# Loads and products ahead of the first P tile in another order, and three quantiser groups moved behind it

## The chip, the cores and the metric

One core of one Trainium2 chip runs the whole program. The metric is the device time of one execution in microseconds (us).

## What is computed

For 8 sequences of 256 tokens with 1024 features (float32), the reference adds two layers to `x`, one after the other:

```python
# layer 0: quantised input, then a routed low-rank layer (4 experts, rank 16)
xq = dequantised x        # 8 thresholds; each has its own delta and zero point
logits = xq @ router_w.T                                  # 4 experts, top 2, softmax over the two
mid = einsum('tf,erf->ter', xq, A)
x = x + einsum('te,teo->to', gates, einsum('ter,eor->teo', mid, B) * 4)
# layer 1: x @ W.T plus a rank-32 part picked by a label, then K, a bias and two low-rank parts
h = einsum('bsi,oi->bso', x, W) + einsum('bsr,or->bso', einsum('bsi,bir->bsr', x, lora_A[label]), B_w) * 0.5
A_eff, B_eff = einsum('bn,nri->bri', gate, LA), einsum('bn,nor->bor', gate, LB)   # 16 LoRAs mixed per sequence
x = x + h @ K + bias + B_eff (A_eff h) + B_shared (A_shared h)
```

## The kernel before

The products that don't depend on `x` are folded first. K' is K plus the shared low-rank update (A_shared by B_shared, rank 32). P is the identity plus W.T times K', 1024 by 1024, kept in SBUF as a high and a low float32r part, so that each product is three passes (high by high, low by high, high by low). With P at hand, each tile of `x` needs one large product and a few thin ones.

**Stages.** (1) The head: small products that mix the LoRA factors. `la` (LoRA A, 4 parts `g`) times the gate matrix gives `aefft` (L814, copied out at L502); `bw` times `aefft` is the bw product, in `cbank` (L824), from which VectorE makes `cbd` (L731); `ab` holds the shared factors, split into a high part by ScalarE (L492) and low parts by VectorE (L712, L713); `k_update` (L796) multiplies them into a ring of three banks and `k_add` (L647) adds each to the loaded K in `kst`; `kp_split` (L431) and `kp_lo_part` (L652) split K'; `v_product` (L806) is `bw` times K'; `lb` (LoRA B, 4 parts, two halves each) times the gate matrix gives 8 table products (L839), which `rows_out` (L488) copies to `tst` and SP stores to `t_dram`. (2) The P loop, `STEPS` = 16 tiles in two halves of 8. In the first half each tile is preceded by a u product (L896, L898), copied out as `ust` (L537). Each tile needs `w_hi` (ScalarE, L424) and `w_lo` (VectorE, L639) of its W tile and ends in `p_hi` (L525) and `p_lo` (L745). K' of the second half is made beside the first half, and split at tile 8. (3) The x loop, 64 slots, two for each tile of 128 tokens by 512 columns.

**The quantiser** runs beside (1) to (3): 8 chunks (sequences) `c` of 8 groups `g`. For each group ScalarE makes the levels (L395) of the *next* group and raises its own (L406); VectorE clips (`value`, L598), makes a mask (L608) and merges (L615); the first group of a chunk has no merge, the last no mask but a `finish` (L620). ScalarE takes |x| once for each chunk (`magnitude`, L387), behind group 1. A raise from group 3 on waits for the merge two groups back, and that of group 1 of a later chunk for all merges of the chunk before. After a chunk, TensorE runs `mid(c)` (L848) in `midbank`, VectorE ranks the experts (`order`, L679 ff.) and makes the gates (`gate`, L695 ff.), TensorE turns them (`gated_turn`, L858) and ScalarE copies the result (`gated_out`, L446).

**What sets the order.** Each engine runs its own instructions in the order written; semaphores join them. All groups stand in a list `ORDER`; the first `AHEAD` are written out by hand in the head and the others are laid into slots (16 of the P loop, 64 of the x loop) by the table `TAKEN`. `DONE[c]` is the slot of a chunk's last group, and `mid`, `order`, `gate` and the turn stand a fixed number of slots behind it (`LAGS`). On ScalarE the groups of slot n+1 come behind `ust(n)` and `p_out(n-1)` of slot n, and ahead of the `w_hi` of slot n+1. On VectorE slot n holds `k_add`, `w_lo`, `p_lo`, the groups of slot n, then ranks and gates. Loads come from SP's queue in the order written, `x` for the quantiser from POOL's (L284).

Of the kernel before, what the change touches and what calls it, by code (L numbers as in the profile page):

```python
# [36 lines left out]
BATCH = 8  # L37
# [3 lines left out]
KT = D // P  # L41
# [17 lines left out]
WARM, WARMUPS = 256, 9  # L59
# [4 lines left out]
def build(nc, a, out_t, itok):  # L64
    arena = [(nc.sbuf_base + 31) // 32 * 32]

    def place(name, shape, dt, at=None, after=0):
# [93 lines left out]
    consts_in, lb_in, ab_in, bw_in, itok_in, alt_in, ra_in = (  # L161
        sem(n) for n in ("consts_in", "lb_in", "ab_in", "bw_in", "itok_in", "alt_in", "ra_in"))
# [12 lines left out]
    t_stored, v_moved = [sem("t_stored0"), sem("t_stored1")], sem("v_moved")  # L175
# [26 lines left out]
    N_CONST = 3  # L202
# [5 lines left out]
    AHEAD = 5  # L208
# [64 lines left out]
    with nc.allow_non_contiguous_dma(reason="rows of 1 KB and small constants"), nc.Block() as block:  # L273

        @block.gpsimd
        def _(pool):

            def quant_input(c):
                if c == 1:
                    pool.wait_ge(lb_in, 16)  # L280
                if c >= 2:
                    pool.wait_ge(levels_made, (c - 1) * G)
                    pool.wait_ge(abs_made, c - 1)
                pool.dma_start(xq[:, c % 2], x_v[c]).then_inc(xq_in[c % 2], 16)  # L284

            for c in range(BATCH):
# [3 lines left out]
        def _(sp):  # L290
            sp.dma_start(small, a["small"]).then_inc(small_in, 16)
            sp.dma_start(ab_raw, a["ab"]).then_inc(ab_in, 16)
            for g in range(NG):
                sp.dma_start(la[:, g], a["la"][:, g]).then_inc(lora_in[g], 16)
            sp.dma_start(bw, a["bw"]).then_inc(bw_in, 16)
            for i in range(KPARTS):
                sp.dma_start(kst[:, i * KO:(i + 1) * KO], k_v[0, :, i * KO:(i + 1) * KO]).then_inc(k_part_in[i], 16)
            for n in range(2):
                sp.dma_start(wst[n], w_v[n]).then_inc(w_in[n], 16)
            sp.dma_start(lb, a["lb"]).then_inc(lb_in, 16)  # L300
            for dst, name in ((bdmask, "bdmask"), (ident_raw, "ident"), (before, "before")):
                sp.dma_start(dst, a[name]).then_inc(consts_in, 16)
            sp.dma_start(itok_sb, itok).then_inc(itok_in, 16)
            sp.dma_start(ra, a["ra"]).then_inc(ra_in, 16)
            sp.wait_ge(itok_in, 16)
            label = [sp.value_load(itok_sb[0:1, b:b + 1], min_val=0, max_val=LAB - 1) for b in range(BATCH)]
            for b in range(BATCH):

                sp.dma_start(alt[b % BG * R:(b % BG + 1) * R, b // BG],
                             a["alt"][bass.ds(label[b], 1)].rearrange("o r i -> (o r) i")).then_inc(alt_in, 16)  # L310
            sp.wait_ge(kp_hi_made, KT)
# [3 lines left out]

            for g in range(NG):
                sp.wait_ge(t_made, 2 * (g + 1))
                sp.dma_start(t_dram[g * RG:(g + 1) * RG].rearrange("r b d -> (r b) d"), tst[0:2 * R, g % 2]).then_inc(t_stored[g % 2], 16)
# [13 lines left out]
            for m in range(2, LOADS):  # L332
# [7 lines left out]
                if m == KT + 2:  # L340

                    for s in range(2):
                        sp.wait_ge(t_stored[s], 16 * NG // 2)
                    sp.wait_ge(kfull, HALVES * KT)
                    sp.wait_ge(v_made, HALVES)
                    for s in range(2):
                        sp.dma_start(tb[R:2 * R, s], tst[3 * R:4 * R, 0]).then_inc(v_moved, 16)
# [35 lines left out]
        def _(act):  # L383
# [5 lines left out]
            def levels(c, g):  # L389

                if g == 0:
                    act.wait_ge(xq_in[c % 2], 16 * (c // 2 + 1))
# [33 lines left out]
            def kp_split(h):  # L426
                for o in range(KT):
                    act.wait_ge(k_sum, h * KT + o + 1)
# [4 lines left out]
            def v_rows(h):  # L433
                act.wait_ge(vfull, h + 1)
                nc.scalar.activation(tst[3 * R:4 * R, 0, h * HALF:(h + 1) * HALF], misc[3 * R:4 * R], ACT.Copy,
                                     scale=LORA1).then_inc(v_made, 1)
# [27 lines left out]
            def bp_out(s):  # L464

                for h in range(HALVES):
                    act.wait_ge(bpfull, h + 1)
                    act.wait_ge(v_moved, 32)
# [13 lines left out]
            def rows_out(n):  # L482
# [3 lines left out]
                if g >= 2 and h == 0:  # L486
                    act.wait_ge(t_stored[g % 2], 16 * (g // 2))
                nc.scalar.activation(tst[0:2 * R, g % 2, h * HALF:(h + 1) * HALF], obank[n % RING][0:2 * R],  # L488
                                     ACT.Copy).then_inc(t_made, 1)

            act.wait_ge(ab_in, 16)
            nc.scalar.activation(ab, ab_raw, ACT.Copy).then_inc(ab_hi_made, 1)  # L492
            act.wait_ge(tables, 1)
            levels(0, 0)
# [531 lines left out]
```

## Time and profile before

| what | us |
|---|---|
| median of 3 runs | 488.16 |
| lowest and highest | 486.01, 490.64 |
| the profiled execution | 489.24 |
| its span in the trace | 487.5 |
| TensorE busy | 471.8 |
| VectorE busy | 391.4 |
| ScalarE busy | 356.6 |

The profile shows one execution. Its engines are PE (TensorE matmuls), PEld (their weight loads), DVE (VectorE), ACT (ScalarE), POOL and SP, which only issues transfers. A float32 matmul shows as two instructions, a float32r one as one. The granted clock (PEclk) is the share of full speed that TensorE's clock was allowed. The time of an execution is some 2 us longer than the span of its trace.

### The profile page before, as it was taken

Reading aid. Unit: us, or ns where it says so; the run is one execution under the profiler, and the core shown is the slowest. Engines: PE = TensorE matmul, PEld = TensorE weight load, DVE = VectorE, ACT = ScalarE, POOL = GpSimd, SP = SyncE. Lnnn points to the kernel's source line nnn. Section 1 sums busy time; section 2 is a strip of 40 time slices with the busy share of each in tenths; the row PEclk is TensorE's granted clock in tenths of the full one; section 3 lists DMA queues with packets and bytes.
Section 4 is the critical chain, followed back from the end, with each engine's and each line's share of the span. In section 5 each row is a group of like instructions: output and inputs, shape, how many; then the busy total and the mean of one; then the engine's idle time right before and its main releaser. Section 6 shows DMA issues by size and latency. Waiting matters only on the chain.

```text
span 487.5 us, 5645 instructions
## 1 busy us (share of the span) xinstructions
PE 471.8 (97%) x2200; PEld 365.7 (75%) x2200; DVE 391.4 (80%) x381; ACT 356.6 (73%) x297; POOL 6.8 (1%) x12
## 2 busy tenths in 40 slices
PE   6989999999889999999999999999999999999896
PEld 5963788887648888787777777787787768767774
DVE  3289978789979989939879989798799994999400
ACT  3779987864978398676699599776899697776001
POOL 0000000001000001000000000000000000000000
PEclk9599999999999999999999999999999999999799
DMA  8975542313301527030441316014214013102002
GB/s 281 422 267 178 171 142 73 90 43 98 107 0 37 181 86 204 13 108 1 151 141 44 108 54 200 38 55 130 108 54 152 0 55 129 56 0 86 1 0 87
DMA packets 35500, 50.61 MB, mean 104 GB/s; under 512 B 26610, under 2 KB 26866, under 8 KB 33074
## 3 DMA queue, kind: packets, MB, share of 16 engines
q1 hardware_dynamic: 34322, 41.87, 26.7%
q0 software_dynamic: 1152, 8.39, 4.8%
q8 instruction: 17, 0.28, 0.2%
q14 instruction: 9, 0.07, 0.1%
HBM read 39.51 MB, written 10.49 MB: 103 GB/s over the span
## 4 chain that ended last, share of the span: by engine, by line
PE 76%; DVE 16%; issue 4%; DMA 2%; ACT 1%; SPq 0%; DVEq 0%; ACTq 0%
PE bank L965 10%; PE bank L966 10%; PE bank L967 10%; DVE val L615 7%; PE bank L848 6%; PE bank L942 5%; PE bank L874 5%; PE bank L917 5%; PE bank L913 5%; PE bank L914 4%; PE bank L896 3%; DVE inside L608 3%; PE bank L814 3%; DVE val L598 2%; DMA la<-la_in 2%
## 5 line engine op out<-in xcount | busy, mean ns | idle before, releaser
L406 ACT ACTIVATE val<-level,shift,small 128x2048 f32<-128x2048 int16 x64 | 133.8, 2091 | 16.3 <-DVE val L615 16.2
L615 DVE COPY_PREDICATED val<-inside,val 128x2048 f32<-128x2048 uint8 x56 | 141.3, 2523 | 0.3
L395 ACT ACTIVATE level<-xq,inv 128x2048 int16<-128x2048 f32 x64 | 127.9, 1998 | 2.0 <-DMA xq<-xt_in 1.4
L598 DVE TENSOR_SCALAR val<-val,width,unshift 128x2048 f32<-128x2048 f32 x64 | 86.0, 1347 | 22.7 <-ACT val L406 22.4
L965 PE MATMUL bank<-p_hi,x_hi 128*128 128x512 f32 x256 | 102.5, 401 | 0.0
L966 PE MATMUL bank<-p_lo,x_hi 128*128 128x512 f32 x256 | 100.4, 392 | 0.0
L967 PE MATMUL bank<-p_hi,x_lo 128*128 128x512 f32 x256 | 100.4, 392 | 0.0
L608 DVE TENSOR_SCALAR inside<-absx,thr 128x2048 uint8<-128x2048 f32 x56 | 71.4, 1285 | 7.1 <-ACT absx L387 7.1
L965 PEld LDWEIGHTS bank<-p_hi,x_hi 128*128 128x128 f32 x256 | 48.5, 189 | 17.6 <-issue 8.8
L966 PEld LDWEIGHTS bank<-p_lo,x_hi 128*128 128x128 f32 x256 | 48.4, 189 | 10.5 <-issue 0.5
L967 PEld LDWEIGHTS bank<-p_hi,x_lo 128*128 128x128 f32 x256 | 48.3, 189 | 10.5
L913 PE MATMUL bank<-kp_hi,w_hi 128*128 128x512 f32 x128 | 50.8, 397 | 1.8 <-DVE kp_lo L652 1.8
L917 PE MATMUL bank<-kp_hi,w_lo 128*128 128x512 f32 x128 | 50.4, 393 | 0.0
L914 PE MATMUL bank<-kp_lo,w_hi 128*128 128x512 f32 x128 | 49.9, 390 | 0.0
L848 PEld LDWEIGHTS bank<-ra,val 128*128 128x128 f32 x256 | 31.5, 202 | 3.0 <-DVE val L620 1.7
L848 PE MATMUL bank<-ra,val 128*128 128x68 f32 x256 | 31.5, 284 | 1.3 <-DVE val L620 1.3
L942 PE MATMUL bank<-tb,zt 128*128 128x512 f32 x64 | 32.7, 599 | 0.0
L896 PE MATMUL bank<-aefft,wst 128*128 128x256 f32 x128 | 29.1, 380 | 2.2 <-ACT ust L537 2.2
L874 PE MATMUL bank<-xs,ub 128*64 128x256 f32 x128 | 29.3, 382 | 0.0
L896 PEld LDWEIGHTS bank<-aefft,wst 128*128 128x128 f32 x128 | 24.1, 190 | 6.9 <-issue 3.4
L913 PEld LDWEIGHTS bank<-kp_hi,w_hi 128*128 128x128 f32 x128 | 24.1, 188 | 6.3 <-issue 2.0
L917 PEld LDWEIGHTS bank<-kp_hi,w_lo 128*128 128x128 f32 x128 | 24.0, 188 | 5.2
(91 smaller groups left out, 477.4 us busy)
## 6 DMA issues: line engine op xcount, KB each, us to landing
xq<-xt_in POOLq DMA_DIRECT2D x8, 1024.0 KB, 5.8
xs<-xt_in SPq DMA_DIRECT2D x8, 1024.0 KB, 4.9
out_t<-ost SPq DMA_DIRECT2D x16, 512.0 KB, 3.0
wst<-w_in SPq DMA_DIRECT2D x14, 512.0 KB, 3.6
la<-la_in SPq DMA_DIRECT2D x4, 512.0 KB, 10.4
kst<-k_in SPq DMA_DIRECT2D x4, 512.0 KB, 13.9
lb<-lb_in SPq DMA_DIRECT2D x1, 2048.0 KB, 18.7
kst<-k_in SPq DMA_DIRECT2D x1, 2048.0 KB, 7.9
```

Of the source, the lines that this page charges most:

```text
L395: nc.scalar.activation(level[:, g % 2], xq[:, c % 2], ACT.Copy, scale=inv[:, g:g + 1]).then_inc(levels_made, 1)
L406: nc.scalar.activation(val[:, turn(c, g)], level[:, g % 2], ACT.Relu, bias=shift[:, g:g + 1], scale=par[:, 1, g:g + 1]).then_inc(raised, 1)
L598: nc.vector.tensor_scalar(v, v, width[:, g:g + 1], unshift[:, g:g + 1], ALU.min, ALU.add).then_inc(valued, 1)
L608: nc.vector.tensor_scalar(inside[:, g % 2], absx, thr[:, g - 1:g], None, ALU.is_le).then_inc(masked, 1)
L615: nc.vector.copy_predicated(val[:, acc(c)], inside[:, g % 2], val[:, turn(c, g)]).then_inc(merged, 1)
L848: last = mm(midbank[:, t * RT:(t + 1) * RT], val[:, acc(c), k, t * P:(t + 1) * P], ra[:, k], start=k == 0, stop=k == KT - 1)
L913: mm(obank[n % RING], w_hi[side(n)][:, o], kp_hi[:, o], start=o == 0, stop=False)
L914: mm(obank[n % RING], w_hi[side(n)][:, o], kp_lo[:, o], start=False, stop=False)
L917: last = mm(obank[n % RING], w_lo[side(n)][:, o], kp_hi[:, o], start=False, stop=o == KT - 1)
L965: mm(o, x_hi[:, s, k, at], p_hi[:, h, k], start=False, stop=False)
L966: mm(o, x_hi[:, s, k, at], p_lo[:, h, k], start=False, stop=False)
L967: last = mm(o, x_lo[:, s, k, at], p_hi[:, h, k], start=False, stop=False)
```

## The change

- **SP's queue.** Before: `ab`, `la`, `bw`, K in 4 parts, two W tiles, `lb` in one transfer, masks and constants, `itok`, `ra`. After: `itok`, `la`, `bw`, `ab`, `bdmask`, `lb` in 4 parts, K in 4 parts, W tile 0, `x` of chunk 0 (from POOL's queue before), `ident`, W tile 1, `before`, `ra`. The stores of table rows 0 and 1 stand ahead of the 8 `alt` loads, 2 and 3 behind them; all stood behind the second K load. POOL loads `x` of chunk 1 when the `alt` loads are in, not `lb`.
- **TensorE.** The bw product comes ahead of the K updates, each of its parts waiting only for its piece of `aefft`. Table products 0 and 1 follow it, then three updates, then one table product between updates, and `v_product` last. The warm-up products are 7, not 9, and the 3 and 4 among the updates are gone.
- **ScalarE.** `aefft` first, then the split of `ab`, then `kp_split(0)` with a `rows_out` ahead of each piece; behind them `w_hi(0)`, the identity, and then the quantiser: group 0, `v_rows(0)`, |x|, group 1, `w_hi(1)`, the levels of group 2.
- **VectorE.** `cbd`, all `k_add`, `kp_lo`, `w_lo(0)`, then groups 0 and 1 with their masks and merge, then `w_lo(1)`.
- **Groups.** `AHEAD` is 2, not 5. The entries of `TAKEN` for slots 0 to 17 stay; those behind take 42 groups in 55 slots, not 39. So the last slots of the chunks (`DONE`) go from 2, 7, 16, 27, 39, 50, 61, 72 to 4, 9, 20, 31, 41, 52, 62, 72, and `mid` from slots 4, 9, 18, 29, 41, 52, 62, 73 to 6, 11, 22, 33, 43, 54, 63, 73.
- **Table rows.** `tst` holds all four row groups (32 partitions farther down for the second pair), so `rows_out` no longer waits for a store. `v_rows` writes straight into both slots of `tb` (two activations instead of one, and a wait for stores 0 and 1), and the two transfers that moved it there are gone.

```diff
-WARM, WARMUPS = 256, 9
+WARM, WARMUPS = 256, 7
-    AHEAD = 5
+    AHEAD = 2
@@ POOL @@
                 if c == 1:
-                    pool.wait_ge(lb_in, 16)
+                    pool.wait_ge(alt_in, 16 * BATCH)
-            for c in range(BATCH):
+            for c in range(1, BATCH):
                 quant_input(c)
@@ SP @@
             sp.dma_start(small, a["small"]).then_inc(small_in, 16)
-            sp.dma_start(ab_raw, a["ab"]).then_inc(ab_in, 16)
+            sp.dma_start(itok_sb, itok).then_inc(itok_in, 16)
             for g in range(NG):
                 sp.dma_start(la[:, g], a["la"][:, g]).then_inc(lora_in[g], 16)
             sp.dma_start(bw, a["bw"]).then_inc(bw_in, 16)
+            sp.dma_start(ab_raw, a["ab"]).then_inc(ab_in, 16)
+            sp.dma_start(bdmask, a["bdmask"]).then_inc(bdmask_in, 16)
+            for g in range(NG):
+                sp.dma_start(lb[:, g], a["lb"][:, g]).then_inc(lb_in[g], 16)
...
+            for g in range(2):
+                table_rows(g)
             for b in range(BATCH):
                 sp.dma_start(alt[b % BG * R:(b % BG + 1) * R, b // BG],
...
+            for g in range(2, NG):
+                table_rows(g)
@@ ScalarE @@
             def kp_split(h):
                 for o in range(KT):
+                    if h == 0:
+                        rows_out(o)
                     act.wait_ge(k_sum, h * KT + o + 1)
...
             def v_rows(h):
                 act.wait_ge(vfull, h + 1)
-                nc.scalar.activation(tst[3 * R:4 * R, 0, h * HALF:(h + 1) * HALF], misc[3 * R:4 * R], ACT.Copy,
-                                     scale=LORA1).then_inc(v_made, 1)
+                for g in range(2):
+                    act.wait_ge(t_stored[g], 16)
+                for s in range(2):
+                    last = nc.scalar.activation(tb[R:2 * R, s, h * HALF:(h + 1) * HALF], misc[3 * R:4 * R], ACT.Copy, scale=LORA1)
+                last.then_inc(v_made, 1)
...
+            act.wait_ge(ab_in, 16)
+            nc.scalar.activation(ab, ab_raw, ACT.Copy).then_inc(ab_hi_made, 1)
+            kp_split(0)
+            weight_hi(0)
+            act.wait_ge(ident_in, 16)
+            nc.scalar.activation(ident, ident_raw, ACT.Copy).then_inc(ident_made, 1)
+            act.wait_ge(tables, 1)
+            levels(0, 0)
+            raise_levels(0, 0)
+            v_rows(0)
             magnitude(0)
+            levels(0, 1)
+            raise_levels(0, 1)
+            weight_hi(1)
             levels(0, 2)
-            weight_hi(0)
-            kp_split(0)
-            quant(*ORDER[2])
...
@@ VectorE @@
+            for o in range(KT):
+                k_add(0, o)
+            kp_lo_part(0)
+            weight_lo(0)
+            value(0, 0)
+            mask(0, 1)
+            mask(0, 2)
+            value(0, 1)
+            merge(0, 1)
             weight_lo(1)
-            quant(*ORDER[3])
-            quant(*ORDER[4])
@@ TensorE @@
+            pe.wait_ge(bw_in, 16)
+            for o in range(KT):
+                pe.wait_ge(afree, o // 2 + 1)
+                last = mm(cbank[:, 0:BATCH * R], bw[:, o], aefft[:, o], start=o == 0, stop=o == KT - 1)
+            last.then_inc(cfull, 1)
+            def table_product(n):
+                g, h = divmod(n, HALVES)
+                pe.wait_ge(lb_in[g], 16)
+                if n >= RING:
+                    pe.wait_ge(t_made, n - RING + 1)
+                mm(obank[n % RING][0:2 * R], gm, lb[:, g, h * HALF:(h + 1) * HALF], start=True, stop=True).then_inc(tfull, 1)
+            table_product(0)
+            table_product(1)
             pe.wait_ge(ab_lo_made, 2)
             for o in range(3):
                 k_update(0, o)
-            for o in range(3, 6):
+            for o in range(3, KT):
+                table_product(o - 1)
                 k_update(0, o)
-            keep_warm(3)
-            for o in range(6, KT):
-                k_update(0, o)
-            keep_warm(4)
+            table_product(KT - 1)
             v_product(0)
```

## Rows read from the trace of the kernel before

**Rows 1.** Busy time by stretch: length, PE, PEld, DVE, ACT, POOL, clock, DMA, GB/s
```profile
0.00:50.00 50.00, 43.42 (x153) 30.23 (x153) 30.41 (x41) 36.97 (x38) 1.76 (x6) 0.86 0.78 288
50.00:142.00 92.00, 88.79 (x417) 72.83 (x416) 79.45 (x71) 71.35 (x57) 2.02 (x2) 1.00 0.32 91
202.00:412.10 210.10, 210.10 (x1048) 159.91 (x1048) 179.98 (x159) 169.74 (x130) 1.59 (x3) 1.00 0.28 89
412.10:454.80 42.70, 41.45 (x185) 30.72 (x184) 42.21 (x38) 27.96 (x23) 0.00 (x0) 1.00 0.11 40
```

**Rows 2.** The same view around the la product
```profile
9.30:12.70 3.40, 1.68 (x15) 1.72 (x16) 2.43 (x2) 2.01 (x2) 0.00 (x0) 0.99 1.02 407
12.70:26.30 13.60, 13.60 (x58) 12.91 (x58) 3.05 (x3) 10.89 (x13) 0.00 (x0) 0.50 1.03 422
```

**Rows 3.** TensorE in order of time: start, us, what, [idle before it and its releaser]
```profile
1.20 6.42 PE L784 MATMUL bank<-warm 128*128 128x256 f32 x18 [1.20 <-DVE warm L655]
11.02 12.40 PE L814 MATMUL bank<-gmix,la 128*128 128x64 f32 x64 [3.40 <-DMA la<-la_in]
...
35.86 7.03 PE L806 MATMUL bank<-kst,bw 128*128 128x512 f32 x16
42.82 7.22 PE L839 MATMUL bank<-lb,gmix 128*64 128x512 f32 x16
49.97 3.72 PE L896 MATMUL bank<-aefft,wst 128*128 128x256 f32 x16
```

**Rows 4.** Transfers of the page: count, KB each, median us to landing
```profile
la<-la_in SPq DMA_DIRECT2D x4, 512.0 KB, 10.4
...
alt<-alt_in SPq DMA_DIRECT2D x8, 128.0 KB, 2.6
```

**Rows 5.** ScalarE in order of time, in the head
```profile
40.19 1.04 ACT L424 ACTIVATE w_hi<-wst 128x1024 fp32r<-128x1024 f32 x1
41.14 1.99 ACT L395 ACTIVATE level<-xq,inv 128x2048 int16<-128x2048 f32 x1
43.03 2.08 ACT L406 ACTIVATE val<-level,shift,small 128x2048 f32<-128x2048 int16 x1
45.14 0.59 ACT L435 ACTIVATE tst<-bank 32x512 f32<-32x512 f32 x1
...
57.47 0.37 ACT L537 ACTIVATE ust<-bank 128x256 f32<-128x256 f32 x1
```

**Rows 6.** VectorE in order of time, slot 0 and the start of slot 1
```profile
57.60 1.35 DVE L598 TENSOR_SCALAR val<-val,width,unshift 128x2048 f32<-128x2048 f32 x1
58.87 1.28 DVE L608 TENSOR_SCALAR inside<-absx,thr 128x2048 uint8<-128x2048 f32 x1
60.06 2.47 DVE L615 COPY_PREDICATED val<-inside,val 128x2048 f32<-128x2048 uint8 x1
62.43 0.68 DVE L647 TENSOR_TENSOR kst<-bank,kst 128x512 f32<-128x512 f32 x1
...
64.81 0.69 DVE L745 TENSOR_TENSOR p_lo<-bank,p_hi 128x512 fp32r<-128x512 f32 x1 [0.57 <-ACT p_hi L525]
```

**Rows 7.** VectorE in order of time, slots 8 to 10
```profile
142.00 4.90 DVE L652 TENSOR_TENSOR kp_lo<-kst,kp_hi 128x512 fp32r<-128x512 f32 x8 [2.50 <-ACT kp_hi L431]
...
154.68 1.24 DVE L639 TENSOR_TENSOR w_lo<-wst,w_hi 128x1024 fp32r<-128x1024 f32 x1
...
161.27 1.21 DVE L639 TENSOR_TENSOR w_lo<-wst,w_hi 128x1024 fp32r<-128x1024 f32 x1
```

**Rows 8.** The chain that ended last: start, us, what; mid(1) and mid(6)
```profile
154.24 3.52 PE bank L848 x32
...
408.57 3.54 PE bank L848 x32
```

**Rows 9.** VectorE's first rank step of chunk 6, and TensorE's mid(7)
```profile
412.13 0.17 DVE L679 COPY lg<-bank 128x8 f32<-128x8 f32 x1 [5.84 <-PE bank L848]
...
454.84 5.71 PE L848 MATMUL bank<-ra,val 128*128 128x68 f32 x32 [1.29 <-DVE val L620]
```

## What I expected before the change was run

> **What bounds the kernel now.** I read the busy time by stretch first [rows 1]. Until 50 us TensorE is busy 43.4 of 50 us, but much of that is filler or slow work. From 50 to 142 us (first half of the P tiles) it idles 3.2 us, from 202 to 412 us not at all. So time won before the first P tile is kept only if VectorE and ScalarE keep pace later: VectorE works 79.5 of 92 us and then 180.0 of 210.1 us, and in the last stretch, to 454.8 us, 42.2 of 42.7.
>
> The chain of waits shows the same: la product, `k_update`, bw product, `v_product`, table products, then the P tiles and x tiles, with VectorE's quantiser taking over three times: about 90 to 142 us, at the step into the second half, and from 412 us. The last needs care: `mid(6)` ends at 412.1, VectorE takes the ranks at 412.13 and works without a gap through chunk 7, and `mid(7)` starts at 454.84 after a 1.29 us wait [rows 8, 9]. What VectorE gives away early it must find again.
>
> **The head, before.** The warm-ups are 18 instructions in 6.4 us; TensorE waits 3.4 us for `la`, whose transfers stand behind `ab` and beside the first `x`; the la product takes 12.40 us [rows 3]. The granted clock is 0.50 from 12.7 to 26.3 us, the lower level (1.2 GHz), under that product and part of the next [rows 2]. `v_product` takes 7.0, table products 7.2, and the first P tile's u product begins at 49.97 [rows 3]. ScalarE's `ust(0)` ends at 57.8 [rows 5]; VectorE enters the P loop at 57.60 [rows 6].
>
> **The change, part by part.**
>
> *Transfers.* `la` is now third on SP's queue, without `ab` (0.8 MB) ahead or `x` (1 MB) beside it. At 407 to 422 GB/s [rows 2] 0.52 MB takes 1.3 us. Before, its median was 10.4 us to landing; a light 128 KB load takes 2.6 [rows 4]. I put the four parts at about 5.5, 7.5, 9 and 10.3 us (slower at first, estimate), bw 11.6, ab 13.5, lb 15 to 19, K 20 to 24, w0 25, x0 27.5. Nine warm-ups less two are 14 instructions, ending about 6.5. So the la product starts at 6.5, not 11.02, and is no longer held by data but by itself.
>
> *la product.* 64 instructions at 0.19 us are 12.4; in the 1.68 us at full clock (11.02 to 12.70) some 14 ran [rows 2, 3], 0.11 to 0.12 each, so 7.3 us. Bounds: ends 13.8 if the clock holds, 18.9 if it is low throughout. I take a drop after some 3.5 us (31 done, 33 at 0.194): end 16.4. The clock fell after a pause and 1.7 us of this product, and did not return in the 10 us of it that followed.
>
> *bw product, factors.* The bw product is 16 instructions of the shape that takes 3.72 us in the u product [rows 3], 7.4 at half clock: half of each, end 22. `ab` goes behind `aefft` on ScalarE and its low parts on VectorE, ready at 21.5, so they hide behind it. Two table products (0.45 x 2 each) and three updates bring `k_sum(1)` to 23.5.
>
> *Table products between the updates.* Each step is one product (0.90) and one update (0.22), 1.12 us; VectorE's add (0.6) fits, and ScalarE's `rows_out` (0.5) with `kp_hi` (0.6) just does. Eight steps end `kp_split(0)` at 31. The 16 instructions that followed `v_product` (7.2 us) now fill what warm-ups filled. `v_product` runs 29.6 to 36.5. On SP two `t_dram` stores, and the waits for `t_made` 2 and 4, now stand before the eight `alt` loads (issued in 3.9 us, 2.6 to landing [rows 4]); with stores at 26.5 these land about 33, before the first P tile needs them. `x` of chunk 1 waits for them on POOL and is not wanted before 79.
>
> *ScalarE becomes the head's bound.* From 31.0 its queue holds, by start-to-start times of [rows 5]: `w_hi(0)` 1.0, ident 0.3, levels and raise (0,0) 4.0, wait for `v_product` 0.3, the two `v_rows` 1.2, |x| 1.8, (0,1) 4.0, `w_hi(1)` 1.0, levels (0,2), (0,3) and raise (0,2) 5.9, together 19.5: raised at 50.5, `ust(0)` at 50.9. VectorE therefore enters the loop at 50.5 instead of 57.60: **-7.1 us**. TensorE does its first P tile from 36.6 to 46.8 and then waits 4 us for `ust(0)`, where before `ust(0)` ended 2 us early. That wait is new, and the clock may fall in it: the second u product then takes 6.8 instead of 3.7 us, and `p_lo(0)` starts at 58.4 instead of 57.5 (before: 64.81 [rows 6]). I take the middle: **-6.9**.
>
> *First half of the loop.* VectorE and ScalarE hold each other: a raise waits for the merge two groups back, the next `w_hi` stands behind it, and `w_lo` behind that. A middle group costs VectorE 4.8 us (57.60 to 62.43 [rows 6]). The groups of slots 1 to 7 are now (0,3) to (1,4) instead of (0,6) to (1,7). Step by step I get slot 2 2.2 us longer (two whole groups instead of a last and a first), slot 3 2.2 shorter, slot 4 4.7 shorter, slot 5 3.6 longer (raise (1,1) and |x| wait for the end of chunk 0, and `w_hi(6)` behind both), slots 6 and 7 2.5 and 1 shorter. Sum -4.6: `kp_lo` of the second half starts at 131 instead of 142.00 [rows 7]. Shift **-11.5**.
>
> *Into the second half.* Before, slot 8 held (2,0), (2,1): 154.68 less 142.00, 4.9 of `kp_lo` and 0.6 of `p_lo`, 7.2 us [rows 7]. Now it holds (1,5), (1,6) and the gates of chunk 0: 9.7 and 1.1, so +3.5. Slot 9 holds (1,7) with the finish instead of (2,2): 6.2 for 4.8, +1.4. So `w_lo(9)`, which began at 161.27, begins at 154.7, and the tile behind it starts at 156 instead of 163.5. Worse, `mid(1)` (3.52 us, at 154.24 under such waiting [rows 8]) moves from slot 9 to slot 11, where nothing hides it. TensorE's lead falls from 7.4 to **-3.8 us**. I keep -2 and -6 as bounds: some twenty waits were laid out by hand.
>
> *Long stretch, 202 to 412.* TensorE idles nowhere. VectorE must now do three more groups (14.6 us) in it, with 30.1 us idle before [rows 1]. `mid(6)` stands one slot later, which gives 3.8 more (eleven slots lie between 412.1 and the 453.55 at which TensorE began to wait [rows 8, 9]), beside some 2.3 us by which chunk 6 was early. I cost it at nothing; without that cover it is up to 8.5 us (a rival).
>
> *The end.* `mid(6)` ends one slot later, 415.9 less the lead. Then VectorE's chain to `mid(7)` is 42.7 (412.13 to 454.84 [rows 9]) less the value of (7,0), now taken before the ranks, 1.25: 41.5. `mid(7)` comes at 457.4 less the lead, against 454.84: **+2.6 us**. TensorE reaches it 4 us early, waits, and runs it at low clock, as before (5.71 us [rows 9] against 3.54 for `mid(6)` [rows 8]).
>
> **Sum.** -3.8 + 2.6 = -1.2 on a span of 487.5, so 488.0 against the profiled execution's 489.24. That execution lies 1.1 above the median 488.16, so on the median's scale the forecast is **487.0 us**.
>
> **Rivals.**
>
> *The clock stays up in the la product.* TensorE no longer pauses before it. The Trainium skill (TensorE: Matmul & The Clock Gate, "What's actually happening") says that the engine is throttled by default and that recent activity releases it, so an engine without a gap would stay fast. Against: this product did not lift the clock in 10 us without a pause [rows 2]. Then it ends at 13.8, the bw product at 17.5, the K parts (20 to 24) set the updates, `kp_split` ends at 27.7, and all is 3.3 us earlier: 483.7.
>
> *The head's gain is kept.* The second half hides `mid(1)` after all and VectorE fills its idle time so well that the end pays nothing: -7.1, 481.1. For it: 30.1 us of idle time. Against: the 42.7 us chain at the end has no idle time to give.
>
> *VectorE can't carry the three groups: slower.* Its idle time before 412 us lies behind ScalarE, which waits for TensorE's events in slot order. With R of it recovered, chunk 6 ends at 406.3 - 3.8 + 14.6 - R, and `mid(6)` needs it at 412.4 - 3.8; it decides below R = 8.5. With R = 2: +6.5, 493.5. For it: three more groups are half of all its idle time there [rows 1].
>
> *Nothing moves.* If `la` lands near 10 us after all, the la product ends near 20 and everything 3.5 us later: 490.5, the same by measurement.
>
> **How the numbers follow.** Likeliest case 0.45, its own range 485 to 490; clock held 0.18; gain kept 0.12; VectorE overloaded 0.15; nothing moves 0.10. Range to the other cases: 481.5 to 493. About 1% (4.9 us) is what a measurement can tell from no change. Faster by more: the kept gain, a third of the held clock, a little of the likeliest, 0.24. Slower by more: most of the overload and a rest, 0.17. Between: 0.59.
>
> **What would show it.** The la product starts at 6 to 7 us and ends near 16; `kp_split(0)` ends near 31; TensorE waits some 4 us for `ust(0)` before 51; `kp_lo` of the second half starts near 131; TensorE waits at tiles 10 and 11; `mid(7)` waits some 4 us behind VectorE. It is wrong if TensorE waits at `mid(4)` to `mid(6)`, or if `ust(0)` comes before 47 or after 54.

## The result, and the profile after

The median of 20 runs is 492.39 us (489.71 to 496.64), that of the kernel before, run beside it 20 times, 488.72. The ratio is 1.0074 [1.0048, 1.0100]: the change makes the kernel slower by 0.7%. The time lies inside my range and within the 1% that I had called the likeliest outcome, but outside the 485 to 490 us of my likeliest case, and on the other side of the old time than the 487.0 us forecast. The profiled execution of after takes 491.64 us with a span of 489.9 (before: 489.24 and 487.5), so the trace shows 2.4 us of the loss; the sum below is made on the spans.

The page of the kernel after, part 1: busy time, its share, instructions of each engine.

```profile
PE 467.9 (96%) x2182; PEld 358.7 (73%) x2182; DVE 391.8 (80%) x381; ACT 358.0 (73%) x299; POOL 6.0 (1%) x11
```

Busy time by stretch, kernel after (columns as in [rows 1]; the clock is the third number from the end):

```profile
0.00:50.00 50.00, 43.52 (x180) 28.11 (x180) 24.21 (x36) 32.62 (x39) 1.09 (x5) 0.99 0.89 319
50.00:142.00 92.00, 90.57 (x411) 73.98 (x412) 80.55 (x74) 70.11 (x61) 1.88 (x2) 0.97 0.28 75
142.00:202.00 60.00, 53.34 (x257) 43.43 (x257) 50.16 (x56) 43.39 (x37) 0.00 (x0) 0.97 0.28 84
202.00:412.00 210.00, 210.00 (x1024) 158.64 (x1020) 193.70 (x167) 179.75 (x135) 3.02 (x4) 1.00 0.29 94
```

Against [rows 1]: the head's granted clock is 0.99 and no longer 0.86, and VectorE has 24.2 us of work in the first 50 us, not 30.4, because three groups went behind. It does them in the long stretch, 193.7 us of 210 where it had 180.0 of 210.1, and TensorE is still busy in all of it. The loss sits in the third line, the second half of the P tiles: 6.7 us idle of 60. (Before, TensorE was busy 59.2 us of the same 60.)

The four longest waits of TensorE, kernel after: us in total, times, longest.

```profile
PE bank L901 <- ACT ust L547: 4.4, 1, 4.4
PE bank L863 <- DVE mg L712: 3.9, 1, 3.9
PE bank L853 <- DVE val L630: 3.6, 1, 3.6
PE bank L938 <- DVE bet_lo L762: 1.4, 1, 1.4
```

The first is the wait for `ust(0)`, the second the gates of chunk 0 at the step into the second half, the third `mid(7)`, the fourth the entry to the x loop (L938, the first product behind the P tiles). TensorE in order of time, kernel after: start, us, what, and in brackets the idle time before it with its releaser.

```profile
5.92 7.25 PE L818 MATMUL bank<-gmix,la 128*128 128x64 f32 x64
13.01 3.67 PE L824 MATMUL bank<-aefft,bw 128*128 128x256 f32 x16
...
23.16 1.07 PE L832 MATMUL bank<-lb,gmix 128*64 128x512 f32 x2
24.16 0.50 PE L800 MATMUL bank<-ab 96*128 96x512 f32 x1
24.59 1.07 PE L832 MATMUL bank<-lb,gmix 128*64 128x512 f32 x2
...
29.89 7.13 PE L810 MATMUL bank<-kst,bw 128*128 128x512 f32 x16
36.98 3.69 PE L901 MATMUL bank<-aefft,wst 128*128 128x256 f32 x16
...
51.37 5.81 PE L901 MATMUL bank<-aefft,wst 128*128 128x256 f32 x16 [4.43 <-ACT ust L547]
...
156.39 0.50 PE L918 MATMUL bank<-kp_hi,w_hi 128*128 128x512 f32 x1 [0.81 <-DVE w_lo L649]
...
162.08 3.68 PE L853 MATMUL bank<-ra,val 128*128 128x68 f32 x32
189.88 0.50 PE L938 MATMUL bank<-p_hi,bet_hi 128*128 128x512 f32 x1 [1.45 <-DVE bet_lo L762]
...
456.18 7.09 PE L853 MATMUL bank<-ra,val 128*128 128x68 f32 x32 [3.64 <-DVE val L630]
```

The la product takes 7.25 us where it took 12.40 [rows 3], with no pause ahead of it. The line at 162.08 is `mid(1)`, the one at 456.18 `mid(7)`, which takes 7.09 us where it took 5.71 [rows 9]. VectorE in order of time, kernel after:

```profile
21.99 2.57 DVE L657 TENSOR_TENSOR kst<-bank,kst 128x512 f32<-128x512 f32 x4 [1.75 <-DMA kst<-k_in]
...
50.86 1.34 DVE L608 TENSOR_SCALAR val<-val,width,unshift 128x2048 f32<-128x2048 f32 x1 [1.74 <-ACT val L417]
...
58.57 0.69 DVE L749 TENSOR_TENSOR p_lo<-bank,p_hi 128x512 fp32r<-128x512 f32 x1 [1.10 <-ACT p_hi L535]
...
131.10 4.90 DVE L662 TENSOR_TENSOR kp_lo<-kst,kp_hi 128x512 fp32r<-128x512 f32 x8 [1.47 <-ACT kp_hi L444]
...
147.15 1.22 DVE L649 TENSOR_TENSOR w_lo<-wst,w_hi 128x1024 fp32r<-128x1024 f32 x1
...
155.12 1.22 DVE L649 TENSOR_TENSOR w_lo<-wst,w_hi 128x1024 fp32r<-128x1024 f32 x1
...
163.43 1.22 DVE L649 TENSOR_TENSOR w_lo<-wst,w_hi 128x1024 fp32r<-128x1024 f32 x1 [3.50 <-ACT w_hi L435]
...
172.54 1.23 DVE L649 TENSOR_TENSOR w_lo<-wst,w_hi 128x1024 fp32r<-128x1024 f32 x1 [5.18 <-ACT w_hi L435]
```

VectorE is 6.7 us ahead of before at 50.86 (57.60 in [rows 6]), 10.9 us ahead at `kp_lo` (142.00 in [rows 7]), and 6.2 us ahead at `w_lo(9)` (155.12 for 161.27). Then it idles 3.50 and 5.18 us while slots 10 to 12 hold one group between them; slots 13 to 15 hold one group each.

Two starts of TensorE that the sum below needs, first the entry to the x loop in the kernel before, in order of time, then `mid(6)` in the chain of the kernel after that ended last:

```profile
191.04 0.39 PE L933 MATMUL bank<-p_hi,bet_hi 128*128 128x512 f32 x1
```
```profile
411.21 3.54 PE bank L853 x32
```

**Where the 2.4 us come from.** Three starts of TensorE carry the sum, each after less before. Entry to the x loop: 189.88 against 191.04 in the trace of before, so 1.16 us early. `mid(6)`: 411.21 against 408.57; it stands one slot of 3.8 us later, and 3.8 less 1.16 is 2.64, just what is seen. `mid(7)`: 456.18 against 454.84, +1.34. It then runs 1.38 us longer, and what follows it is 0.3 us shorter: 1.34 + 1.38 - 0.3 = 2.4.

### The profile page after: what moved, and what is told of

It reads as the page before. It is cut to its first block, busy times and chain, and to the rows that moved or that the text cites. A ratio compares the mean times of both kernels' runs of the same rounds, so it can differ in the third digit from the quotient of the medians.

```text
span 489.9 us, 5626 instructions
## 1 busy us (share of the span) xinstructions
PE 467.9 (96%) x2182; PEld 358.7 (73%) x2182; DVE 391.8 (80%) x381; ACT 358.0 (73%) x299; POOL 6.0 (1%) x11
## 4 chain that ended last, share of the span: by engine, by line
PE 59%; DVE 21%; ACT 8%; issue 7%; DMA 3%; SPq 1%; ACTq 0%; DVEq 0%
PE bank L970 10%; PE bank L972 10%; PE bank L971 10%; DVE val L625 9%; PE bank L853 6%; PE bank L947 5%; PE bank L879 5%; DVE val L608 3%; DVE inside L618 3%; DMA kst<-k_in 3%; ACT level L406 3%; ACT val L417 3%; PE bank L968 1%; PE bank L875 1%; PE bank L810 1%
## 5 line engine op out<-in xcount | busy, mean ns | idle before, releaser
L970 PEld LDWEIGHTS bank<-p_hi,x_hi 128*128 128x128 f32 x256 | 48.4, 189 | 16.7 <-issue 7.9
L853 PEld LDWEIGHTS bank<-ra,val 128*128 128x128 f32 x256 | 32.9, 209 | 5.7 <-DVE val L630 4.1
L853 PE MATMUL bank<-ra,val 128*128 128x68 f32 x256 | 32.9, 292 | 3.6 <-DVE val L630 3.6
L901 PE MATMUL bank<-aefft,wst 128*128 128x256 f32 x128 | 31.3, 400 | 4.4 <-ACT ust L547 4.4
L901 PEld LDWEIGHTS bank<-aefft,wst 128*128 128x128 f32 x128 | 25.6, 202 | 9.8 <-issue 5.8
L649 DVE TENSOR_TENSOR w_lo<-wst,w_hi 128x1024 fp32r<-128x1024 f32 x14 | 17.2, 1227 | 16.4 <-ACT w_hi L435 16.3
```

The lines of the kernel that those rows point to most:

```text
L853: last = mm(midbank[:, t * RT:(t + 1) * RT], val[:, acc(c), k, t * P:(t + 1) * P], ra[:, k], start=k == 0, stop=k == KT - 1)
L901: mm(ubank, wst[n % 2][:, o], aefft[:, o], start=o == 0, stop=False)
L970: mm(o, x_hi[:, s, k, at], p_hi[:, h, k], start=False, stop=False)
```

## The experiments

The expectations call theory 1 the account by place: the three groups moved behind make VectorE late at the step into the second half and at the end, and that takes back what the head gives. Its rivals put the loss on the clock or on the head. The measured times below are medians of five rounds, and ratios are to the kernel before on the same chip; the kernels themselves ran on several chips, so the ratios compare them more safely than the times. Starts and durations come from one profiled execution of each.

**The groups moved, the head not.** In the kernel before, only the three groups leave the head.

```diff
-    AHEAD = 5
+    AHEAD = 2
@@ ScalarE @@
-            quant(*ORDER[2])
...
-            quant(*ORDER[3])
...
-                if n == NG - 1:
-                    quant(*ORDER[4])
@@ VectorE @@
-            quant(*ORDER[2])
...
-            quant(*ORDER[3])
-            quant(*ORDER[4])
```

> The kernel before with the old order of its head, but with only two groups of the quantiser ahead of the first P tile (AHEAD 2); the three others move into the slots behind, as in the changed kernel. Theory 1 (the loss comes from the moved groups: mid products without cover in the second half, and the chunk-6 ranks one slot later at the end): the first u product still begins near 50 us, and ScalarE and VectorE are free 5 us earlier than before, but the end pays 2.6 us and a low clock: ratio to the kernel before 1.004 to 1.012 (490.5 to 494.5 us). Theory 2 (the loss comes from the new order of transfers and products in the head): ratio 0.997 to 1.002.

Measured: 498.46 us, 1.0179 [1.0148, 1.0210], span 497.9. The direction is as expected, the size above what I had expected. TensorE's waits, old head with two groups ahead (columns as above):

```profile
PE bank L851 <- DVE mg L697: 4.0, 1, 4.0
PE bank L841 <- DVE val L616: 3.7, 1, 3.7
...
PE bank L926 <- DVE bet_lo L751: 1.5, 1, 1.5
```

They are the waits of the kernel after, to 0.1 us, except the one for `ust(0)`. So the late waits belong to the move of the groups, not to the new order in the head. Both kernels have the same slots, so their starts compare one to one: `mid(1)` comes at 169.52 here and 162.08 after, `mid(6)` at 418.70 and 411.21, `mid(7)` at 463.69 and 456.18. That is 7.4, 7.5 and 7.5: with the slots equal, the lead that these two traces have at 160 us lasts to the end and nothing takes it back. The size is less sure: the profiled execution is one of the two slowest of six, and its first u product starts at 51.01, 1.0 us later than in the kernel before, though the head is as before up to there. By the ratios and the medians (498.46 and 492.39) the new head gives 5 to 6 us, and the move costs 9.3 us (498.46 less the 489.14 of the kernel before beside it); by the spans the move costs 10.4.

**The groups back, the new head kept.** In the kernel after, `AHEAD` is 5 again and the three groups are written out behind the levels of group 2 (ScalarE) and `w_lo(1)` (VectorE).

```diff
-    AHEAD = 2
+    AHEAD = 5
...
+            for k in range(2, 5):
+                quant(*ORDER[k])
```

> The changed kernel with its new head, but with five groups ahead of the first P tile again (AHEAD 5, the three groups written out behind the levels of group 2), so that every group and every mid product stands in the slot it had before. Theory 1: ScalarE carries 12.1 us more before the copy of the first u product, which ends at 63 instead of 51.2 us (57.8 before); nothing behind it is worse than before, so about 5 us are lost: ratio 1.008 to 1.013 (493 to 495 us), with no extra wait at the last mid product. Theory 2: ratio 1.005 or more too, but with the loss before 50 us in TensorE's first products; the trace tells the two apart.

Measured: 495.92 us, 1.0104 [1.0062, 1.0146]. TensorE in order of time, new head with five groups ahead:

```profile
65.04 5.74 PE L905 MATMUL bank<-aefft,wst 128*128 128x256 f32 x16 [16.71 <-ACT ust L549]
```

Three groups in ScalarE's queue ahead of `ust(0)` make TensorE wait 16.7 us instead of 4.4. In return the waits for the gates and for `bet_lo` are gone, and that for `mid(7)` is 1.4 us, as in the kernel before: once more they go with the groups. So the new head needs the three groups out of it. Its ScalarE queue is already full from 31.3 to 50.85 us (0.49 us idle), because groups 0 and 1, which the old head did under the la product (10.66 to 18.80 us in the trace of before), now stand there too. As the queue is laid out here, the new order pays only together with the move.

**Only the end of the table as before.** In the kernel after, the long stretch takes three groups more at slots 21, 31 and 42, so that the last slots fall as before.

```diff
-    TAKEN += [(i + 1) * rest // room - i * rest // room for i in range(room)]
+    TAKEN += [(i + 1) * (rest - 3) // room - i * (rest - 3) // room for i in range(room)]
+    for i in (21, 31, 42):
+        TAKEN[i] += 1
```

> The changed kernel with the 42 groups of the long stretch laid out so that the slots from 43 on hold what they held before (the three extra groups go to slots 21, 31 and 42): the last groups of chunks 5, 6, 7 are in slots 50, 61, 72, and the mid product of chunk 6 is in slot 62 instead of 63. Theory 1: the chain at the end starts one slot earlier, the last mid product comes about 2.5 us earlier, TensorE waits about 1 us there instead of 3.6: 2.5 to 4 us faster than the changed kernel, ratio to the kernel before 0.999 to 1.003 (488 to 490 us). Rival (VectorE can't carry the three groups in time): TensorE waits at the mid products of chunks 3 to 6, no gain against 492.4 us, ratio 1.006 or more.

Measured: 492.09 us, 1.0062 [1.0036, 1.0088], which can't be told from the kernel after. The gain that theory 1 promised is not there. TensorE in order of time, tail slots as before:

```profile
295.59 0.71 PE L865 MATMUL bank<-ident,mg 128*128 128x128 f32 x4 [2.16 <-DVE mg L714]
...
456.68 5.10 PE L855 MATMUL bank<-ra,val 128*128 128x68 f32 x32 [1.26 <-DVE val L632]
```

The denser slots make a new wait of 2.16 us in the long stretch, so `mid(6)` comes only 0.8 us earlier (410.44), though it stands a slot of 3.8 us earlier; the wait explains 2.2 of the 3.0 us missing. And `mid(7)` comes no earlier at all: from the end of `mid(6)` (413.98, with its 3.54 us) VectorE's chain is again 42.7 us, as in the kernel before, and not 41.4, because the value of (7,0) again stands behind the ranks. So this table gives back the slot, but loses most of it in a new wait and the rest in the chain. It can't show what the one slot of `mid(6)` is worth; that part of theory 1 rests on the starts in the traces alone.

**Filler products ahead of `mid(7)`.** In the kernel after, 14 products that nobody reads stand where TensorE waits for VectorE's last chunk.

```diff
-                pe.wait_ge(q_made, c + 1)
-                pe.wait_ge(ra_in, 16)
                 if c:
                     pe.wait_ge(mgt_made, c)
+                if c == BATCH - 1:
+                    for _ in range(14):
+                        mm(midbank, ones, p_hi[:, 0, 0], start=True, stop=True)
+                pe.wait_ge(q_made, c + 1)
+                pe.wait_ge(ra_in, 16)
```

> The changed kernel with 14 filler products (512 columns, 0.23 us each, 3.2 us) on TensorE in its 3.6 us wait for the last quantised chunk. Theory 1: the granted clock stays at full through the last mid product, which takes 3.5 instead of 7.1 us: ratio to the kernel before 0.998 to 1.003 (487.5 to 490 us), 3 to 4 us faster than the changed kernel. Rival: the clock falls in the mid product all the same, because that product itself is too light; then 0 to 1 us is gained (491.5 to 492.4 us).

Measured: 488.02 us, 0.9989 [0.9961, 1.0016]: 4.4 us less than the kernel after. TensorE in order of time, `mid(7)` behind fillers:

```profile
456.85 3.79 PE L856 MATMUL bank<-ra,val 128*128 128x68 f32 x32 [0.47 <-DVE val L630]
```

It starts no earlier (456.85), but takes 3.79 us, not 7.09. Fillers don't shorten the wait; they keep the granted clock up through it. In the kernel after, the stretch of `mid(7)` has this line (columns as in [rows 1]):

```profile
456.20:463.30 7.10, 7.10 (x33) 7.10 (x34) 0.00 (x0) 0.00 (x0) 0.00 (x0) 0.50 0.01 2
```

0.50 is the lower of the two levels, 1.2 GHz, throughout. So at the end the clock costs 3.3 us of the 7.09 in this product alone.

**The step into the second half mended.** In the kernel after, slot 8 takes one group, slots 10 and 12 one instead of none, slot 13 none. The last group of chunk 1 then lies in slot 10, not 9, and its `mid`, `order`, `gate` and turn follow one slot closer behind it, so that `mid(1)` stays in slot 11.

```diff
-    LAGS = [(2, 3, 4, 5, 6)] * 2 + [(2, 4, 5, 6, 7)] * (BATCH - 4) + [(1, 2, 3, 4, 5)] * 2
-    TAKEN = [1, 1, 2, 1, 2, 2, 1, 1, 2, 1, 0, 1, 0, 1, 1, 1, 1, 1]
+    LAGS = [(2, 3, 4, 5, 6), (1, 2, 3, 4, 5)] + [(2, 4, 5, 6, 7)] * (BATCH - 4) + [(1, 2, 3, 4, 5)] * 2
+    TAKEN = [1, 1, 2, 1, 2, 2, 1, 1, 1, 1, 1, 1, 1, 0, 1, 1, 1, 1]
```

> The changed kernel with four entries of the slot table altered around the step into the second half: slot 8 holds one group instead of two, slot 10 one instead of none, (2,1) stands in slot 12 instead of 13, and the mid product of chunk 1 stays in slot 11. VectorE then reaches the gates of chunk 0 and the low part of the tile 5 us earlier. Theory 1 (the head's lead is lost at this step, by the moved groups): TensorE's 3.9 us wait for the gates, the waits at tiles 10 and 11 and the 1.4 us before the beta products go away, and 5 to 6.5 us are won over the changed kernel: ratio to the kernel before 0.993 to 0.998 (485.5 to 488 us). Rival (the lead is given back in the long stretch or at the end whatever the second half does, since VectorE is the bound there): below 2 us won, ratio 1.003 or more.

Measured: 486.72 us, 0.9953 [0.9918, 0.9988], 5.7 us less than the kernel after. TensorE in order of time, mended slots:

```profile
156.76 3.79 PE L853 MATMUL bank<-ra,val 128*128 128x68 f32 x32 [1.04 <-DVE val L630]
...
183.03 0.50 PE L938 MATMUL bank<-p_hi,bet_hi 128*128 128x512 f32 x1 [0.17 <-DVE bet_lo L762]
...
449.37 6.45 PE L853 MATMUL bank<-ra,val 128*128 128x68 f32 x32 [3.68 <-DVE val L630]
```

The x loop begins at 183.03, 6.85 us earlier than after and 8.0 earlier than before, and `mid(7)` is 6.8 us earlier too. So four entries of the table held back nearly all of the head's gain. It was lost ahead of the x loop, and what arrives there stays: theory 1's first place is shown. The wait of 3.7 us before `mid(7)` is still there.

**Filler products ahead of the second u product.** In the kernel after, 17 products behind the first P tile, under the wait for `ust(0)`.

```diff
                     pe.wait_ge(w_in[n % 2], 16 * (n // 2 + 1))
+                    if i == 1:
+                        pe.wait_ge(ones_made, 1)
+                        pe.wait_ge(t_made, NG * HALVES)
+                        for _ in range(17):
+                            mm(obank[3], ones, kp_hi[:, 0], start=True, stop=True)
                     if i:
```

> The changed kernel with 17 filler products (3.9 us) in TensorE's 4.4 us wait for the copy of the first u product. The second u product should then run at the full clock (3.7 instead of 5.8 us) and the low part of the first P tile begin 1.1 us earlier. Theory 1: VectorE's order bounds what follows, so the gain is 1 us at most: ratio to the kernel before 1.004 to 1.008. If the low clock there were the larger part of the loss, 2 us or more would be won: ratio 1.003 or less.

Measured: 490.81 us, 1.0046 [1.0016, 1.0075], 1.6 us less than the kernel after. The two intervals overlap, so the runs alone don't prove a gain; the trace shows what the fillers do. TensorE in order of time, fillers before the second u product:

```profile
51.21 3.72 PE L906 MATMUL bank<-aefft,wst 128*128 128x256 f32 x16 [0.55 <-ACT ust L547]
```

The product takes 3.72 instead of 5.81 us, and `kp_lo` of the second half starts 1.3 us earlier (129.82), `mid(7)` 1.35 (454.83). Some two thirds of the saved product arrive.

**Fillers in the kernel before.** Six of them ahead of `mid(7)`, with the same reordering of waits as above.

```diff
+                if c == BATCH - 1:
+                    for _ in range(6):
+                        mm(midbank, ones, p_hi[:, 0, 0], start=True, stop=True)
```

> The kernel before with 6 filler products (1.4 us) in the 1.3 us wait for the last quantised chunk. Its last mid product ran at the low clock too (5.7 us against 3.5). Theory 1: it runs at the full clock and 2 to 3.5 us are won: ratio to the kernel before 0.993 to 0.996. If the filler only shifts the work behind it: 0.999 to 1.002.

Measured: 487.18 us, 0.9976 [0.9949, 1.0003]. That is between my two expectations, and the interval just touches no change; the trace shows the mechanism. The chain that ended last, kernel before with fillers:

```profile
454.77 3.67 PE bank L851 x32
```

The kernel before had the same loss at this place, 5.71 us for 3.67 (it waits 1.29 us there [rows 9]). So the change only made an old loss larger, by the 1.38 us of the sum.

**All three mends together**: mended slots and both fillers, on the kernel after.

> The changed kernel with the altered slot table, the filler products in the wait for the first u copy and those ahead of the last mid product, together. Theory 1: the gains add, some 5.5 + 4.4 + 0.5 us off 492.4: 481 to 483.5 us, ratio to the kernel before 0.984 to 0.989. Rival: the parts overlap, because all end in the same wait of TensorE for VectorE: 485 us or more, ratio 0.992 or more.

Measured: 478.56 us (478.27 to 481.32, six runs), 0.9812 [0.9766, 0.9857]: 1.9% faster than the kernel before and 13.8 us faster than the kernel after, where the three edits alone gave 5.7, 4.4 and 1.6, together 11.7. The mean granted clock is 1.000. TensorE in order of time, all three:

```profile
51.67 3.72 PE L909 MATMUL bank<-aefft,wst 128*128 128x256 f32 x16 [0.57 <-ACT ust L547]
...
447.51 3.79 PE L856 MATMUL bank<-ra,val 128*128 128x68 f32 x32 [0.48 <-DVE val L630]
```

Both products run at the full clock. The time is 2 us below the sum of the parts and below the 481 to 483.5 us expected. The medians of the parts are uncertain by about 1 us each, and in the trace of the mended slots alone the low clock cost more than in that of the kernel after: the second u product took 6.73 us (5.81 after), and from the end of `mid(7)` to the end of the span it was 27.8 us (26.6 after, 25.6 here). There the fillers had more to win.

**The old head in the mended loop.** The head of the kernel before (its transfers, its order, two groups ahead), the mended slots, 14 fillers at `mid(7)`, none at the second u product.

```diff
-    AHEAD = 5
+    AHEAD = 2
...
+    TAKEN = [1, 1, 2, 1, 2, 2, 1, 1, 1, 1, 1, 1, 1, 0, 1, 1, 1, 1]
```

> The old head with two groups ahead, the altered slot table and the filler products ahead of the last mid product (the kernel with all three improvements, but with the order of the head as before; the filler in the wait for the first u copy has no wait to fill and is left out). Theory 1 (the new order of the head is itself worth 7 us once the slots behind it fit): 6 to 9 us slower than the kernel with all three, ratio to the kernel before 0.994 to 0.999 (486 to 489 us). Rival (the new order of the head gives little, the gain is all from slots and clock): below 3 us slower, ratio 0.987 or less.

Measured: 487.29 us, 0.9964 [0.9936, 0.9993], 8.7 us more than with all three mends. TensorE in order of time, old head in the mended loop:

```profile
161.12 5.01 PE L844 MATMUL bank<-ra,val 128*128 128x68 f32 x32 [1.05 <-issue]
```

This is `mid(1)`, and not all of the 8.7 us is the new head. At the second P tile the kernel with all three mends is 7.1 us ahead (55.59 against 62.70), at the tile ahead of `mid(1)` 6.2 (148.03 against 154.24). Then the clock is 0.50 here from 163.4 to 170.2 us: `mid(1)` takes 5.01 us for 3.76 and the tile behind it 7.28 for 5.28, and the lead at the entry to the x loop is 9.1. So the new order, with its filler, is worth some 6 to 7 us once the loop takes it, and in this trace the rest is clock.

**The pause before the la product filled.** In the kernel before, 16 warm-ups instead of 9.

```diff
-WARM, WARMUPS = 256, 9
+WARM, WARMUPS = 256, 16
```

> The kernel before with 16 warm-up products instead of 9, so that TensorE has no pause between them and the la product. If the pause made the clock fall under the la product, that product now takes 7.3 instead of 12.4 us and ends near 18.5; since ScalarE's queue holds two groups until 18.8 and K lands at 18 to 21, only 1 to 3 us reach the first P tile: ratio to the kernel before 0.994 to 0.999. If the product is too light to hold the clock, it takes 11 to 12.5 us as before: ratio 0.999 to 1.002.

Measured: 486.05 us, 0.9938 [0.9912, 0.9964]. TensorE in order of time, kernel before without the pause, and then the granted clock in the second part of the la product (columns as in [rows 1]):

```profile
1.20 9.84 PE L784 MATMUL bank<-warm 128*128 128x256 f32 x32 [1.20 <-DVE warm L655]
11.16 7.33 PE L814 MATMUL bank<-gmix,la 128*128 128x64 f32 x64
...
21.27 6.57 PE L824 MATMUL bank<-aefft,bw 128*128 128x256 f32 x16 [2.03 <-ACT aefft L502]
...
47.03 3.72 PE L896 MATMUL bank<-aefft,wst 128*128 128x256 f32 x16
```
```profile
14.00:18.00 4.00, 4.00 (x39) 4.00 (x37) 1.35 (x1) 3.97 (x3) 0.00 (x0) 1.00 1.03 411
```

The same product on the same data, started 0.14 us later, takes 7.33 us instead of 12.40, because the 3.40 us pause [rows 3] is gone. The low clock is not gone but later and shorter: it is 0.50 from 20.3 to 27.1 us, behind a wait of 2.03 us for `aefft`, and the bw product takes 6.57 us for 4.46. The u product of the first P tile starts 2.9 us earlier and the kernel is 3.1 us faster. One constant gives 0.6%, nearly as much as the change costs.

## Why the prediction was right in its picture and wrong in its sign

Two terms of the sum failed. The lead into the x loop was put at -3.8 us and measured -1.16, because the count stopped at `mid(1)`; and the low clock in `mid(7)` was put at no change and measured +1.4 us. The details, in order of time:

**The la product: wrong, and it didn't show.** I let the clock fall after 3.5 us. It stayed at 1.00: the product ran from 5.92 to 13.17. The step that failed was the reading of [rows 2 and 3]. There the product had run 10 us at 0.50 without lifting the clock, and I concluded that it also couldn't hold it. The run without the pause, with the same product at 1.00 throughout, shows that the pause lowered it. The Trainium skill (TensorE: Matmul & The Clock Gate, "What's actually happening") says that recent activity releases an engine that is throttled by default. That agrees with the 7.25 and 7.33 us here. Why 10 us of the same product at 0.50 did not raise the clock, no run here settles.

**The updates: two errors that cancelled.** I gave a step 1.12 us. It took 1.43 (23.16, 24.59, 26.02 in the rows above): a table product alone is 1.00, the update 0.43, where I had 0.90 and 0.22. And the head came early to the updates: the la product ended 3.2 us before my 16.4, the bw product at 16.7 and not at 22. Most of that was lost waiting (1.23 us for the split of `ab`, 0.99 for the first sum, which needed K, landed at about 22 us): the first sum was done near 22.7, where I had 23.5. The longer steps took the rest. `kp_split(0)` ended at 31.4, near the 31 predicted, by luck. The rival with the held clock had the right mechanism and the wrong price: it kept the 1.12 us step.

**ScalarE bounds the head: right.** `ust(0)` starts at 50.85 (predicted to end at 50.9), VectorE enters the loop at 50.86 (50.5), TensorE waits 4.43 us (4), `p_lo(0)` is at 58.57 (57.5 or 58.4). The drop of the clock that I left open happened: 5.81 us for 3.72. With fillers there `mid(7)` came 1.35 us earlier; by the medians it is 1.6 us, which is not clear of the noise.

**First half of the loop: right in its total, in part by luck.** `kp_lo` is at 131.10 (131), but the single slots are not as forecast: slot 4 was 0.1 us longer and not 4.7 shorter, slot 5 0.4 shorter and not 3.6 longer (starts of `w_lo` in the two traces). The step into the second half is right slot by slot: slot 8 3.4 us longer (3.5), slot 9 1.4 (1.4), `w_lo(9)` at 155.12 (154.7), the tile behind it at 156.39 (156), `mid(1)` uncovered in slot 11.

**Into the x loop: too small.** I forecast a lead of 3.8 us there and stopped counting at `mid(1)`. Behind `mid(1)` it was near that: TensorE's lead was 10.9 us at the first tile of the second half, 9.2 and 6.8 at the two tiles after the wait for the gates, and 3.2 to 3.6 at the three tiles behind `mid(1)`. But it fell to 2.9 at the last tile and to 1.16 at the entry to the x loop. Of this, the last wait, 1.45 us for `bet_lo`, is the piece that I can name in the trace: I had not followed slots 13 to 15, where VectorE has a group in each, as before, and now the gates of chunk 1 too (slot 13, before slot 11), and reaches `bet_lo` late after idling 8.7 us a little earlier. The mended table shows it: 0.17 us of wait and a lead of 8.0.

**Long stretch: right.** No wait of TensorE, with 13.7 us more work of VectorE; the rival in which it can't carry the groups is refuted in this kernel. The run with three groups more in it shows how near the limit lies: 2.16 us of wait at once.

**The end: the slot right, the clock missed.** `mid(7)` came 2.5 us later relative to the lead (1.34 and 1.16), for 2.6 predicted. But my sum said low clock, as before, 5.71 us. Before, only part of `mid(7)` was slow after a 1.29 us wait; after 3.64 us all of it was. I had the wait of 4 us in the text and gave it no price. That term is +1.4 us. The +2.5 itself is read from the starts and not shown by a run of its own: the tail-slot run took back the slot and paid 2.16 us of it in a new wait. How early chunk 6 was done doesn't matter in either: VectorE idles 3.92 us ahead of the ranks of chunk 6 in the kernel after and 5.86 us in the tail-slot run, in both for `mid(6)`, which comes when TensorE reaches its slot.

**The sum.** Predicted -3.8 + 2.6 = -1.2. Measured on the spans -1.16 + 2.5 + 1.4 - 0.3 = +2.4. The 3.6 us between them are 2.6 of lead and 1.4 of clock, less the rest and rounding. By the medians the change costs 3.7 us rather than 2.4: the profiled execution of after lies 0.75 below its median and that of before 0.5 above.

## What to carry to other kernels

When work is moved behind a point, follow the queue of each engine to the next place where the engines meet in lock step, and then to the one after it: here a lead of 10.9 us at 132 us was down to 1.2 at 190 us, by four entries of a table that fitted the old head. Price a wait of TensorE as its length and, on top, what may run behind it at half clock; filler products under a wait that couldn't be avoided gave 4.4 us before `mid(7)`, and some 1.5, not clear of the noise, before the second u product. Undo the halves of a change apart: the costly half (moved groups, +9.3 us) and the useful one (order of the head, 5 to 7 us) hid each other.

## What the runs showed of the hardware

- **The same product kept a full granted clock and did not raise a low one.** The la product took 7.25 and 7.33 us with TensorE busy ahead of it, and 12.40 us behind a 3.40 us pause, 10 us of it at 0.50. `mid(7)` took 3.79 us behind fillers and 7.09 behind a 3.64 us wait.
- **A short wait can cost the clock, but its length alone doesn't tell.** Behind 1.29 and 1.26 us of wait `mid(7)` took 5.71 and 5.10 us for 3.54; with 0.5 us it took 3.7 to 3.8. 1.04 us before `mid(1)` in the mended kernel did no harm (3.79 us); 1.05 us at the same place behind the old head was followed by 0.50 (5.01 us). And in the kernel before, waits of 2.23 us (at 123.8) and 1.82 us (at 142.8) left the clock at 1.00. With the three mends the mean granted clock went from 0.978 to 1.000.
- **In the kernel after, the clock also fell between 147 and 157 us** (0.83 in the row below, columns as in [rows 1]), behind the wait for the gates of chunk 0. The tile behind it took 6.71 us, against 5.36 at full clock in the mended kernel. It cost nothing more here: the next tile waits 0.81 us for `w_lo(9)` all the same.

```profile
147.00:157.00 10.00, 8.51 (x32) 6.59 (x33) 9.93 (x9) 5.67 (x5) 0.00 (x0) 0.83 0.43 131
```
